# A graph network on one core: the back state turned through DRAM by VectorE, the engines' orders written anew, and some matmul operands moved by 32 bytes

## The chip, the cores and the metric

The kernel runs on 1 core of one Trainium2 chip (trn2), in one launch. The metric is the time of the device in microseconds, the median of its runs. All times below are microseconds (us) unless marked ns.

## What is computed

The input x holds 32 graphs of 256 nodes by 256 features (fp32), with one 256x256 adjacency matrix adj for all. Four layers follow each other, each with a residual and a layer norm over the features:

```
h = x
3 times:  a = adj @ h
          z = sigmoid([a, a] @ w3.T + b3 + h @ u3.T + bu)
          r = sigmoid([a, a] @ w4.T + b4 + h @ u3.T + bu)
          c = tanh([a, a] @ w5.T + b5 + (r * h) @ u5.T + bv)
          h = (1 - z) * h + z * c
x = norm(x + h)
rel = adj.T * (q @ k.T), each row divided by its length;  x = norm(x + rel @ v)     (q, k, v = x @ Wq.T, Wk.T, Wv.T)
x = norm(x + (adj @ x) @ w2 + b2)
x = norm(x + D adj D @ (x @ w3s) + b3s)                  (D = 1 / sqrt of the degrees)
```

## The kernel before

**Arithmetic.** Every fp32 operand of a large matmul is split into two parts of type float32r, hi (a ScalarE copy) and lo (operand minus hi, on VectorE, the functions ending in `_lo`). A product takes three matmuls per 128 rows of contraction: hi by hi, hi by lo, lo by hi. So a bank of PSUM (128x512 fp32) costs 6 matmuls of 512 columns (`base`, `reset`, `update`, `candidate_mixed`, `candidate_reset`: a 128x128 weight, a state of 512 columns streamed), or 12 of 256 columns (`mix`, `keys`, `values`, `relate`, `attend`, `mix_nodes`, `convolve`, where the 256 nodes or features of one graph are streamed). In the names of the profile, out<-a,b, a is what is streamed and b what is loaded as weight.

**Pairs and lanes.** The 32 graphs are worked on in 16 pairs, 512 nodes each. Two lanes are interleaved. The front lane runs two of the three rounds of a pair p (n = 2p and 2p+1 in the code), the back lane the third round of the pair before, q = p - 1, and then, as `main`, the layers of q. One pass of the loop `Fori(2, LAST)` is 13 times the same; a `start` and a `finish` stand around it. In `finish` the last pair's third round and its layers run in the front lane (`last_pair`).

**The state and its turning.** A round needs its state h twice: features on partitions (`feat`, for `base`) and nodes on partitions (`node`, for `mix`). `hand_over_h` leaves the new state of the back lane as `feat`; `turn_h(state_b, ...)` (L677) turns it by 8 TensorE transposes of 128x128 into a PSUM bank, from where `node_hi` (ScalarE) and `node_lo` (VectorE) split it. The front state of the odd rounds and the sum in front of the layers are turned another way: VectorE transposes 32x32 blocks (`turn_state`, `turn_sum_blocks`), SP writes them to a DRAM scratch and reads them back in another order (`move_blocks`, L370 and L373: one write, a wait for its landing, four reads), and `moved_hi` and `moved_lo` split what arrives.

**Order.** Each engine's instructions stand in a list written out by hand in its `body`, `start` and `finish`, and each engine works strictly through its own. They wait for each other by semaphores. SP issues nearly all DMAs, in its own order: `load_front`, `load_blocks`, `keep_input`, `move_sum`, `move_blocks`, `store`. TensorE's list in the loop, end of a pass and beginning of the next: `mix_nodes(main, q, 1, 0 and 1)`, `convolve(main, q, 1, 0)`, `turn_h(state_b, p, 0 and 1)`, `convolve(main, q, 1, 1)`, then `mix(back)`, `mix(front)`, `base(back)`, `reset(back)`. The last layer norm of a pair (`out_sum`, `stats_of(3)`, `moments_of(3)` on VectorE, `inverse_std` on GpSimd, `normalise_rows(3)` on ScalarE, then `store`) runs into the next pass.

**Addresses.** Tensors lie one behind the other in a partition, in the order in which the code declares them, each at a multiple of 32 bytes. Before the change every operand of every matmul starts at a multiple of 128 bytes. The 8 floats of `shift_32` move what is declared behind it by 32 bytes, until `shift_back`.

## Time and profile before

| what | value |
|---|---|
| median of 3 runs | 1224.64 us (1224.62 to 1224.92) |
| the profiled execution's own time | 1224.91 us |
| its span, first to last instruction | 1223.1 us |
| TensorE busy | 1207.9 us, 99% |
| VectorE busy | 1003.4 us, 82% |
| ScalarE busy | 657.5 us, 54% |
| GpSimd busy | 192.8 us, 16% |
| granted TensorE clock, mean | 0.998 |
| DMA | 66.93 MB, 18.2% of 16 engines on SP's queue |

The engines run beside each other, so busy shares don't add up; what counts is the engine whose work ends last at each place. PE is TensorE's matmuls, PEld its weight loads (they run beside the matmuls), DVE is VectorE, ACT ScalarE, POOL GpSimd, SP SyncE with its DMA queue. Matmuls overlap in the profile: the time one costs is the distance to the start of the next, not its duration.

### The profile page before, as it was taken

How to read it: one execution, taken by the hardware profiler on the slowest of the kernel's cores; microseconds unless marked ns; L12 is line 12 of the kernel's file. 1: busy time of each engine (PE TensorE's matmuls, PEld its weight loads, DVE VectorE, ACT ScalarE, POOL GpSimd, SP SyncE). 2: the span in 40 equal slices, each digit the busy share in tenths (PEclk: the TensorE clock that was granted, in tenths of full speed). 3: DMA queues.
4: the chain of work that ended last, by engine and by line, in shares of the span. 5: the costliest groups of instructions: out<-in, count | busy, mean ns of one | idle time of the engine just before them, and what ended most of it. 6: DMA issues, size and time to landing. Idle time of an engine off the chain costs nothing.

```text
span 1223.1 us, 21243 instructions
## 1 busy us (share of the span) xinstructions
PE 1207.9 (99%) x7454; PEld 1089.1 (89%) x7454; DVE 1003.4 (82%) x2220; ACT 657.5 (54%) x1179; POOL 192.8 (16%) x447
## 2 busy tenths in 40 slices
PE   9999999999999999999999999999999999999997
PEld 7789899898998989899898998989989898998896
DVE  7689788897878978788887888978789787886799
ACT  5455555555555555555555555555555555555542
POOL 1002021110211102012020211102111021120122
PEclk9999999999999999999999999999999999999999
DMA  6020221303113030120402213031130311300001
GB/s 207 18 84 21 63 77 35 103 0 86 51 34 103 0 103 34 46 91 1 119 17 53 84 34 103 0 86 51 34 103 0 103 34 42 95 1 35 1 2 35
DMA packets 105021, 66.93 MB, mean 55 GB/s; under 512 B 65690, under 2 KB 98468, under 8 KB 104996
## 3 DMA queue, kind: packets, MB, share of 16 engines
q1 hardware_dynamic: 104784, 66.08, 18.2%
q0 software_dynamic: 192, 0.52, 0.2%
q8 instruction: 15, 0.25, 0.1%
q14 instruction: 10, 0.08, 0.0%
q10 hardware_dynamic: 20, 0.01, 0.0%
HBM read 35.13 MB, written 23.07 MB: 48 GB/s over the span
## 4 chain that ended last, share of the span: by engine, by line
PE 97%; DVE 2%; POOL 0%; ACT 0%; issue 0%; DVEq 0%; POOLq 0%
PE b_ps L515 41%; PE f_ps L515 31%; PE f_ps L510 15%; PE b_ps L510 7%; PE f_ps L677 1%; PE b_ps L741 1%; PE b_ps L559 0%; PE f_ps L1052 0%; DVE b_stats L1678 0%; DVE f_stats L1678 0%; DVE f_gate L1694 0%; PE b_ps L574 0%; DVE hf_feat L1706 0%; DVE hf_feat L1694 0%; DVE normed L1694 0%
## 5 line engine op out<-in xcount | busy, mean ns | idle before, releaser
L423 POOL TENSOR_TENSOR b_var_eps<-b_moments,eps 128x2 f32<-128x2 f32 x120 | 34.9, 290 | 913.1 <-DVE b_moments L1685 913.0
L1115 ACT ACTIVATE f_cand<-f_ps,bias_c 128x512 f32<-128x512 f32 x66 | 45.6, 691 | 86.0 <-PE f_ps L515 84.3
L425 POOL TENSOR_TENSOR b_rstd<-b_var_eps,neg_half 128x2 f32<-128x2 f32 x120 | 88.2, 735 | 9.4
L1063 ACT ACTIVATE b_rh_hi<-b_ps 128x512 fp32r<-128x512 f32 x90 | 53.7, 596 | 65.5 <-PE b_ps L515 65.5
L1103 ACT ACTIVATE f_gate<-f_ps,bias_r 128x512 f32<-128x512 f32 x66 | 45.4, 688 | 70.7 <-PE f_ps L515 70.7
L1063 ACT ACTIVATE b_a_hi<-normed 128x512 fp32r<-128x512 f32 x60 | 37.9, 632 | 61.3 <-DVE normed L1694 61.3
L515 PE MATMUL f_ps<-adjT_hi,hf_node_hi 128*128 128x256 f32 x264 | 67.3, 287 | 0.5 <-DVE adjT_lo L1481 0.5
L515 PE MATMUL f_ps<-adjT_lo,hf_node_hi 128*128 128x256 f32 x264 | 66.1, 283 | 0.0
L1720 DVE TENSOR_TENSOR b_rh_lo<-b_ps,b_rh_hi 128x512 fp32r<-128x512 f32 x90 | 61.4, 682 | 4.6 <-ACT b_rh_hi L1063 4.4
L1577 DVE TENSOR_TENSOR f_cand<-f_z,f_cand 128x512 f32<-128x512 f32 x66 | 45.5, 689 | 23.0 <-ACT f_cand L1115 23.0
L1561 DVE TENSOR_TENSOR f_gate<-f_gate,hf_feat 128x512 f32<-128x512 f32 x66 | 44.8, 680 | 20.2 <-ACT f_gate L1103 20.2
L1063 ACT ACTIVATE f_a_hi<-f_ps 128x512 fp32r<-128x512 f32 x66 | 39.0, 592 | 40.5 <-PE f_ps L515 40.5
L1555 DVE TENSOR_TENSOR b_a_lo<-b_ps,b_a_hi 128x512 fp32r<-128x512 f32 x30 | 19.4, 687 | 49.2 <-ACT b_a_hi L1063 49.2
L1111 ACT ACTIVATE f_z<-f_ps,bias_z 128x512 f32<-128x512 f32 x66 | 45.1, 685 | 26.6 <-PE f_ps L510 26.6
L1555 DVE TENSOR_TENSOR f_a_lo<-f_ps,f_a_hi 128x512 fp32r<-128x512 f32 x66 | 44.9, 682 | 14.0 <-ACT f_a_hi L1063 14.0
L1182 ACT ACTIVATE result<-result,b_shift,b_rstd 128x256 f32<-128x256 f32 x56 | 30.8, 597 | 46.2 <-POOL b_shift L431 46.2
L1063 ACT ACTIVATE hf_feat_hi<-hf_feat 128x512 fp32r<-128x512 f32 x64 | 38.8, 626 | 25.1 <-DVE hf_feat L1641 22.2
L515 PE MATMUL f_ps<-hf_feat_hi,u3T_hi 128*128 128x512 f32 x132 | 52.0, 394 | 0.1
L515 PE MATMUL f_ps<-f_a_hi,w4T_hi 128*128 128x512 f32 x132 | 51.8, 393 | 0.0
L515 PE MATMUL f_ps<-hf_feat_hi,u3T_lo 128*128 128x512 f32 x132 | 51.8, 392 | 0.0
L515 PE MATMUL f_ps<-f_a_hi,w4T_lo 128*128 128x512 f32 x132 | 51.6, 391 | 0.0
L510 PE MATMUL f_ps<-f_a_hi,w34T_hi 128*128 128x512 f32 x132 | 51.5, 390 | 0.0
(340 smaller groups left out, 4335.7 us busy)
## 6 DMA issues: line engine op xcount, KB each, us to landing
x_front<-in_x SPq DMA_DIRECT2D x16, 512.0 KB, 4.0
x_blocks<-in_x SPq DMA_DIRECT2D x60, 128.0 KB, 2.9
input_t<-hf_feat SPq DMA_DIRECT2D x15, 512.0 KB, 2.9
turn_sum<-normed SPq DMA_DIRECT2D x14, 512.0 KB, 2.7
result<-turn_sum SPq DMA_DIRECT2D x56, 128.0 KB, 2.8
turn_f<-f_gate SPq DMA_DIRECT2D x14, 512.0 KB, 2.7
f_z<-turn_f SPq DMA_DIRECT2D x56, 128.0 KB, 2.8
out<-result SPq DMA_DIRECT2D x14, 512.0 KB, 3.2
```

Of the source, the lines that this page charges most:

```text
L423: pool.tensor_tensor(Y.var_eps[:, g], Y.moments[:, g, :, 1], eps[:], ALU.add).then_inc(Y.s_var, 1)
L425: pool.tensor_tensor(Y.rstd[:, g], Y.var_eps[:, g], neg_half[:], ALU.pow).then_inc(Y.s_rstd, 1)
L510: last = pe.matmul(bank, s, m, start=start and i == 0, stop=stop and i == len(terms) - 1, skip_group_check=True)
L515: return pe.matmul(bank, s, m, start=start, stop=stop, skip_group_check=True)
L1063: return act.activation(dst, src, ACT.Copy)
L1103: act.activation(L.gate[:, k], L.ps0[:, k], ACT.Sigmoid, bias=bias_r[:, k:k + 1]).then_inc(L.s_r, 1)
L1111: act.activation(L.z[:, k], L.ps0[:, k], ACT.Sigmoid, bias=bias_z[:, k:k + 1]).then_inc(L.s_z, 1)
L1115: act.activation(L.cand[:, k], L.ps1[:, k], ACT.Tanh, bias=bias_c[:, k:k + 1]).then_inc(L.s_tanh, 1)
L1555: dve.tensor_tensor(L.a_lo[:, k], L.ps1[:, k], full(L.a_hi[:, k]), ALU.subtract).then_inc(L.s_a_lo, 1)
L1561: dve.tensor_tensor(L.gate[:, k], L.gate[:, k], L.state.feat[:, k], ALU.mult).then_inc(L.s_rh, 1)
L1577: dve.tensor_tensor(L.cand[:, k], L.z[:, k], L.cand[:, k], ALU.mult).then_inc(L.s_zc, 1)
L1720: dve.tensor_tensor(lo[:, g], src, full(hi[:, g]), ALU.subtract).then_inc(done, 1)
```

## The change

The back state is turned like the front one: `turn_state(state_b)` on VectorE, `move_blocks(state_b)` through a scratch of its own on SP, `moved_hi` and `moved_lo` in place of `node_hi` and `node_lo`. `turn_h(state_b)` goes. Its blocks and what comes back lie in the back lane's `kept` and `cand`. The values v of the attention now lie in the back lane's a_hi and a_lo, and the operand x of the two convolutions gets a buffer of its own (it lay there before). adjT, norm_adjT, w2s, w3s, the split sum and the split relation are declared between `shift_32` and `shift_back`. And all engines' lists are written anew, in `body`, `start` and `finish`; the diff shows the loop's where the order around the turned state is, the rest only moves instructions. The front mix no longer waits for the back state to have left its bank, but for the tanh before it.

```diff
--- before.py
+++ after.py
...
-        if by_blocks:
-            self.s_blocks = sem(f"{name}_s_blocks")
-            self.s_written, self.s_moved = sem(f"{name}_s_written"), sem(f"{name}_s_moved")
+        self.s_blocks = sem(f"{name}_s_blocks")
...
-        adjT = split_matrix("adjT")
-        norm_adjT = split_matrix("norm_adjT")
...
-        w2s = split_matrix("w2s")
-        w3s = split_matrix("w3s")
...
 
-        state_f = State(sb, sem, "hf", [P, C, T], [P, G, C, D], True)
-        state_b = State(sb, sem, "hb", [P, C, T], [P, G, C, D], False)
+        state_f = State(sb, sem, "hf", [P, C, T], [P, G, C, D])
...
+        state_b.scratch = scratch("turn_b")
+        state_b.blocks, state_b.moved = quarters(back.kept), quarters(back.cand)
...
 
+        shift_32 = sb("shift_32", [P, 8])
+        adjT = split_matrix("adjT")
+        norm_adjT = split_matrix("norm_adjT")
+        w2s = split_matrix("w2s")
+        w3s = split_matrix("w3s")
+        sum_split = sb("sum_hi", [P, C, T], F32R), sb("sum_lo", [P, C, T], F32R)
+        rel_split = nodes("rel_hi", F32R), nodes("rel_lo", F32R)
+        shift_back = sb("shift_back", [P, 8])
+
         main = Layers(sb, sem, "b", back, per_graph, input_t, s_input_t, 0,
-                      (sb("sum_hi", [P, C, T], F32R), sb("sum_lo", [P, C, T], F32R)), nodes("normed"), nodes("result"),
-                      (nodes("v_hi", F32R), nodes("v_lo", F32R)), (nodes("rel_hi", F32R), nodes("rel_lo", F32R)),
+                      sum_split, nodes("normed"), nodes("result"),
+                      (per_graph(back.a_hi), per_graph(back.a_lo)), rel_split,
                       sb("sq_sum", [P, G, N]), True)
...
         main.sum_blocks, main.sum_moved = (t[:].rearrange("p g c d -> p (g c) d") for t in (main.normed, main.result))
+
+        main.x_hi, main.x_lo = nodes("x_hi", F32R), nodes("x_lo", F32R)
...
             keep_input(0)
+            move_blocks(state_b, 1)
             with sp.Fori(1, LAST) as p:
                 load_front(p + 1)
                 load_blocks(p + 1)
                 keep_input(p)
                 move_sum(main, p - 1)
                 move_blocks(state_f, p)
+                move_blocks(state_b, p + 1)
                 store(main, p - 1)
...
                     pe.wait_ge(main.s_ax_lo, conv(n - 1, 1, k))
-                if pair is not None and later(pair):
-                    pe.wait_ge(state_b.s_node_lo, upto(pair - 1, k))
+                if pair is not None:
+                    pe.wait_ge(front.s_tanh, upto(n - 1, k))
...
             def body(p, q):
 
                 for k in range(2):
+                    mix(front, 2 * p, k, p)
+                for k in range(2):
+                    base(back, q, k)
+                for k in range(2):
                     mix(back, q, k)
                 for k in range(2):
-                    mix(front, 2 * p, k, p)
-                for k in range(2):
-                    base(back, q, k)
-                for k in range(2):
                     reset(back, q, k)
-                candidate_mixed(back, q, 0)
                 for k in range(2):
                     update(back, q, k)
                 candidate_mixed(back, q, 1)
+                candidate_mixed(back, q, 0)
                 for k in range(2):
                     candidate_reset(back, q, k)
                 base(front, 2 * p, 0, p)
                 reset(front, 2 * p, 0)
                 base(front, 2 * p, 1, p)
+                update(front, 2 * p, 0)
                 reset(front, 2 * p, 1)
+                candidate_mixed(front, 2 * p, 0)
+                update(front, 2 * p, 1)
+                candidate_reset(front, 2 * p, 0)
                 candidate_mixed(front, 2 * p, 1)
-                update(front, 2 * p, 0)
-                candidate_mixed(front, 2 * p, 0)
-                candidate_reset(front, 2 * p, 0)
-                update(front, 2 * p, 1)
+                keys(main, q, 0)
                 candidate_reset(front, 2 * p, 1)
-                for k in range(2):
-                    keys(main, q, k)
-                values(main, q, 0)
-                for k in range(2):
-                    relate(main, q, k)
+                keys(main, q, 1)
+                relate(main, q, 0)
+                for k in range(2):
+                    values(main, q, k)
+                relate(main, q, 1)
                 base(front, 2 * p + 1, 0)
-                values(main, q, 1)
+                sum_squares(main, q, 0)
+                for k in range(2):
+                    attend(main, q, k)
+                sum_squares(main, q, 1)
                 base(front, 2 * p + 1, 1)
-                sum_squares(main, q, 0)
-                attend(main, q, 0)
-                sum_squares(main, q, 1)
                 for k in range(2):
                     mix(front, 2 * p + 1, k)
-                attend(main, q, 1)
-                reset(front, 2 * p + 1, 0)
+                mix_nodes(main, q, 0, 0)
+                for k in range(2):
+                    reset(front, 2 * p + 1, k)
+                convolve(main, q, 0, 0)
+                mix_nodes(main, q, 0, 1)
+                update(front, 2 * p + 1, 0)
+                convolve(main, q, 0, 1)
                 candidate_mixed(front, 2 * p + 1, 0)
-                reset(front, 2 * p + 1, 1)
-                mix_nodes(main, q, 0, 0)
-                update(front, 2 * p + 1, 0)
-                mix_nodes(main, q, 0, 1)
-                for k in range(2):
-                    convolve(main, q, 0, k)
                 candidate_reset(front, 2 * p + 1, 0)
+                update(front, 2 * p + 1, 1)
                 candidate_mixed(front, 2 * p + 1, 1)
-                update(front, 2 * p + 1, 1)
                 candidate_reset(front, 2 * p + 1, 1)
...
 
                 for k in range(2):
+                    moved_hi(state_b, q, k, q + 1)
+                input_hi(p, 0)
+                for k in range(2):
                     a_hi(back, q, k)
+                reset_gate(back, q, 0)
                 a_hi(front, 2 * p, 0)
-                reset_gate(back, q, 0)
+                reset_gate(back, q, 1)
                 rh_hi(back, q, 0)
-                reset_gate(back, q, 1)
-                input_hi(p, 0)
                 update_gate(back, q, 0)
                 rh_hi(back, q, 1)
                 update_gate(back, q, 1)
+                a_hi(front, 2 * p, 1)
...
                 conv_ax_hi(main, q, 0, 1)
                 rh_hi(front, 2 * p + 1, 1)
                 update_gate(front, 2 * p + 1, 0)
+                conv_x_hi(main, q, 1, 0)
+                input_nodes_hi(p + 1, 1)
                 candidate(front, 2 * p + 1, 0)
-                conv_x_hi(main, q, 1, 0)
                 update_gate(front, 2 * p + 1, 1)
                 conv_x_hi(main, q, 1, 1)
                 candidate(front, 2 * p + 1, 1)
                 for k in range(2):
                     conv_ax_hi(main, q, 1, k)
                 out_sum(main, q, 0)
-                node_hi(state_b, p, 0, 2 * p + 0 + 1)
-                feat_hi(state_b, p, 0)
-                node_hi(state_b, p, 1, 2 * p + 1 + 1)
-                feat_hi(state_b, p, 1)
-                input_nodes_hi(p + 1, 1)
+                for k in range(2):
+                    feat_hi(state_b, p, k)
                 out_sum(main, q, 1)
                 for k in range(2):
...
 
                 for k in range(2):
+                    moved_lo(state_b, q, k)
+                turn_blocks(p, 0)
+                for k in range(2):
                     a_lo(back, q, k)
                 a_lo(front, 2 * p, 0)
-                reset_h(back, q, 0)
-                turn_blocks(p, 0)
+                input_lo(p, 0)
+                for k in range(2):
+                    reset_h(back, q, k)
                 rh_lo(back, q, 0)
-                reset_h(back, q, 1)
-                input_lo(p, 0)
                 keep(back, q, 0)
+                rh_lo(back, q, 1)
                 residual(main, back, q, q, 0)
-                rh_lo(back, q, 1)
                 turn_blocks(p, 1)
+                keep(back, q, 1)
                 input_lo(p, 1)
                 a_lo(front, 2 * p, 1)
                 candidate_part(back, q, 0)
...
                 candidate_part(front, 2 * p + 1, 0)
-                normalise(main, q, 2, 1)
-                conv_x_lo(main, q, 1, 0)
+                keep(front, 2 * p + 1, 1)
                 hand_over_h(p, 0)
                 conv_x_lo(main, q, 1, 1)
-                fill(main, q, 1, 0)
+                turn_state(state_b, p, 0)
                 candidate_part(front, 2 * p + 1, 1)
-                keep(front, 2 * p + 1, 1)
+                hand_over_h(p, 1)
+                turn_state(state_b, p, 1)
                 conv_ax_lo(main, q, 1, 0)
-                hand_over_h(p, 1)
                 fill(main, q, 1, 1)
                 conv_ax_lo(main, q, 1, 1)
+                input_nodes_lo(p + 1, 0)
                 stats_of(main, q, 3, 0)
-                for k in range(2):
-                    node_lo(state_b, p, k)
-                for k in range(2):
-                    input_nodes_lo(p + 1, k)
-                feat_lo(state_b, p, 0)
                 moments_of(main, q, 3, 0)
-                feat_lo(state_b, p, 1)
+                input_nodes_lo(p + 1, 1)
                 stats_of(main, q, 3, 1)
                 moments_of(main, q, 3, 1)
+                for k in range(2):
+                    feat_lo(state_b, p, k)
...
```

## Rows read from the trace of the kernel before

**Rows 1.** The page: TensorE's line, and the chain that ended last by engine
```profile
PE 1207.9 (99%) x7454; PEld 1089.1 (89%) x7454; DVE 1003.4 (82%) x2220; ACT 657.5 (54%) x1179; POOL 192.8 (16%) x447
...
PE 97%; DVE 2%; POOL 0%; ACT 0%; issue 0%; DVEq 0%; POOLq 0%
```

**Rows 2.** Windows: stretch, us, busy by engine (instructions), granted clock, DMA, GB/s
```profile
498.30:572.65 74.35, 74.35 (x462) 67.19 (x461) 61.64 (x136) 40.96 (x76) 11.90 (x28) 1.00 0.19 56
...
1093.13:1223.10 129.97, 119.58 (x770) 108.10 (x768) 104.74 (x253) 57.23 (x102) 23.30 (x48) 0.99 0.05 17
```

**Rows 3.** Timeline, TensorE: start, duration, line, out<-streamed,weight, form
```profile
499.74 0.28 PE L515 MATMUL b_ps<-adjT_hi,hb_node_hi 128*128 128x256 f32 x1
...
500.70 0.64 PE L515 MATMUL b_ps<-adjT_hi,hb_node_lo 128*128 128x256 f32 x4
...
510.89 0.39 PE L510 MATMUL b_ps<-b_a_hi,w34T_hi 128*128 128x512 f32 x1
...
514.97 0.39 PE L515 MATMUL b_ps<-b_rh_hi,u5T_hi 128*128 128x512 f32 x1
```

**Rows 4.** Timeline, TensorE: 512 columns behind a 256 block, and the end
```profile
578.41 0.40 PE L515 MATMUL b_ps<-hb_feat_hi,u3T_hi 128*128 128x512 f32 x1
...
579.80 0.39 PE L515 MATMUL b_ps<-hb_feat_hi,u3T_hi 128*128 128x512 f32 x1
```

**Rows 5.** Timeline, TensorE: 256 columns behind 512
```profile
553.44 0.28 PE L515 MATMUL b_ps<-adjT_hi,b_a_hi 128*128 128x256 f32 x1
553.55 0.28 PE L515 MATMUL b_ps<-adjT_lo,b_a_hi 128*128 128x256 f32 x1
```

**Rows 6.** Timeline, TensorE: the back state's turning and what follows
```profile
570.35 1.04 PE L677 MATMUL f_ps<-ident,hb_feat 128*128 128x128 f32 x8
571.15 0.36 PE L515 MATMUL b_ps<-w3s_hi,b_rh_hi 128*128 128x256 f32 x1
571.35 0.28 PE L515 MATMUL b_ps<-w3s_lo,b_rh_hi 128*128 128x256 f32 x1
```

**Rows 7.** Timeline, TensorE: the product in full precision at the start
```profile
27.28 1.89 PE L574 MATMUL b_ps<-hb_feat 128*128 128x256 f32 x8
```

**Rows 8.** Timeline, TensorE, ending: convolve behind mix_nodes; in brackets idle time, releaser
```profile
1189.10 0.74 PE L515 MATMUL b_ps<-adjT_hi,b_a_lo 128*128 128x256 f32 x4 [0.22 <-DVE b_a_lo L1720]
1190.62 0.36 PE L515 MATMUL b_ps<-w2s_hi,b_rh_hi 128*128 128x256 f32 x1 [0.78 <-ACT b_rh_hi L1063]
```

**Rows 9.** Timeline, VectorE and SP's queue: the front state's way through DRAM
```profile
534.25 0.70 DVE L1621 STREAM_TRANSPOSE f_gate<-hf_feat 128x512 f32<-128x512 f32 x1
...
534.98 0.34 SPq L370 DMA_DIRECT2D turn_f<-f_gate  x1
537.66 1.73 SPq L373 DMA_DIRECT2D f_z<-turn_f  x4
```

**Rows 10.** The page's DMA issues: KB each, us from issue to landing
```profile
f_z<-turn_f SPq DMA_DIRECT2D x56, 128.0 KB, 2.8
```

**Rows 11.** Timeline, TensorE and ScalarE behind the pass's last candidate_reset
```profile
566.04 0.28 PE L515 MATMUL b_ps<-norm_adjT_hi,b_a_hi 128*128 128x256 f32 x1
...
566.24 0.69 ACT L1115 ACTIVATE f_cand<-f_ps,bias_c 128x512 f32<-128x512 f32 x1
```

**Rows 12.** Groups by line, ScalarE, one pass: busy us, mean ns
```profile
L1063 ACT ACTIVATE b_a_hi<-b_ps 128x512 fp32r<-128x512 f32 x2 | 1.1, 580 | 0.0
```

**Rows 13.** Timeline, VectorE, GpSimd, ScalarE: the last norm, second graph
```profile
575.92 0.75 DVE L1678 BATCH_NORM_STATS2 b_stats<-result 128x6 f32<-128x256 f32 x2
...
577.21 0.19 POOL L423 TENSOR_TENSOR b_var_eps<-b_moments,eps 128x2 f32<-128x2 f32 x1
...
578.64 1.10 ACT L1182 ACTIVATE result<-result,b_shift,b_rstd 128x256 f32<-128x256 f32 x2 [0.25 <-POOL b_shift L431]
```

**Rows 14.** Timeline, TensorE, start: base(back, 0)
```profile
48.39 0.47 PE L515 MATMUL b_ps<-hb_feat_hi,u3T_hi 128*128 128x512 f32 x1 [1.39 <-ACT hb_feat_hi L1063]
```

**Rows 15.** Windows, start: columns as in rows 2
```profile
50.00:53.00 3.00, 3.00 (x10) 2.51 (x11) 1.83 (x3) 0.71 (x2) 0.00 (x0) 0.50 0.01 3
```

879 lines of the change are left out of this document (440 added, 439 removed).

## The prediction, made before the change was run

> **What bounds the kernel now.** I read the page's totals first: TensorE is busy 99% of the span and carries 97% of the chain that ended last [rows 1]. Then the windows by stage: one pass of the loop takes 74.35 us and TensorE is busy for all of it, VectorE for 61.6, ScalarE for 41.0; only the ending (130.0 us, 119.6 busy) has holes [rows 2]. So in the 13 passes the time is the number of matmuls times the spacing of their starts, and nothing else. The timeline gives that spacing (durations overlap, so only starts count): eight matmuls of 256 columns in 0.96 us, 120 ns each; 18 of 512 columns in 4.08 us, 226.7 ns each [rows 3]. [...] A pass holds, by the code, 264 matmuls of 256 columns (three mix calls of two banks, then keys, values, relate, attend, two of mix_nodes, two of convolve: 22 banks of 12) and 180 of 512 (30 products of 6), 31.7 + 40.8 us. The rest of the 74.35 is the back state's turning, the sums of squares and small costs where the length changes: the first six matmuls of 512 columns behind a 256 block take 1.39 us instead of 1.36 [rows 4], and the first of 256 behind a 512 block has a spacing of 0.11 instead of 0.12 [rows 5].
>
> **The change, part by part.**
>
> *The removed transposes.* `turn_h(state_b)` is 8 transposes at the end of a pass: from the first, 570.35, to the next block, 571.15, 0.80 us, and that block's first spacing is 0.20 instead of 0.12 [rows 6]. Together 0.88, less 0.01 for the slightly tighter ones behind it: **-0.87 us a pass**. There is nothing else on TensorE there, so all of it is on the path.
>
> *The addresses.* adjT, norm_adjT, w2s, w3s, sum and relation move to addresses 32 bytes off a multiple of 64; everything else stays on one. In each of main's 256-column products exactly one of the two operands moves: mix, mix_nodes and convolve stream a shifted matrix past an unshifted weight, keys streams the shifted sum, values, relate and attend load a shifted weight. In all 512-column products neither moves. No row has a matmul with operands placed so, so the effect has to be bounded. [...] I take the better row that exists for 256 columns, one step less: 264 x 6.67 = **-1.76 us a pass** (ends -2.85 and +1.76, and 0 is possible).
>
> [...]
>
> *The order.* Lengths change 8 times a pass instead of 6 (base back, reset back, candidate_reset front 1, the base of the odd round twice, reset, update, candidate): 2 x 0.027 less one or two gains of 0.007: **+0.05**. More important is what stands behind `mix(back, 1)`: before, mix and base of other states (5.6 us), now `reset(back, 0)` at once, which needs a_hi and a_lo of the last bank. The nearest row is in the ending, where convolve stands straight behind mix_nodes: four matmuls from 1189.10, 0.74 long, the last lasting about 0.28 and so starting near 1189.56; next start 1190.62 behind one ScalarE copy [rows 8]; less its own 0.12 that is 0.94 us from where TensorE could have gone on. Here bank 0's two products (0.45) fit in, bank 1's start at 0.94 instead of 0.45; then a_lo of bank 1 is due at 1.7 (0.20 from matmul to ScalarE, 0.58 for the copy [rows 11, 12], 0.7 on VectorE, 0.2 to start), where the stream gets at 1.62, and the rest of the product follows it. **+0.57 us a pass** (from 0.4, if the copy is quicker, to 0.75, since `input_hi(p, 0)`, behind `turn_blocks`, now stands ahead of both a_hi on ScalarE). This is a new wait, and behind it in TensorE's list stand only `reset(back, 1)` and the updates, which need the same values.
>
> *The back state through DRAM.* VectorE gets two transposes of 0.70 [rows 9], moved_lo takes node_lo's place: 61.6 + 1.4 = 63 of some 72.5 us, not the bound. Two more terms matter, both against the time at which TensorE gets to `mix(back, 0)`. Let T be the end of a pass's matmuls. From T come mix(front) 24 x 0.12 and base(back) 2.75: T + 5.6 (5.5 with the shift). (i) The turn. The front state's, now: the transpose ends at 534.95, the write is issued at 534.98, the four reads within 1.73 from 537.66, and one lands 2.8 us after its issue [rows 9, 10]: the last at about 541.9, 7.0 us after the transpose. The back's starts when the last candidate_reset ends, 5.8 us before T (566.04; tanh at 566.24 for 0.69 [rows 11]), then candidate_part, hand_over and transpose at 0.6 to 0.7 each, behind conv_x_lo and the other half's transpose: 2.9 to 3.6 us. So it has landed at T + 4.1 to 4.8 and node_hi is there at T + 4.8 to 5.5. (ii) ScalarE's queue. `moved_hi(back)` is behind `normalise_rows(q, 3)`. Now these end at T + 7.1 (578.64 + 1.10 against 572.65), because VectorE gets to the last stats only at 575.92 [rows 13]; from there to the end it is 3.8 us. In the new order only input_nodes_lo, stats and moments stand before it: T + 1.2, so moved_hi can start at about T + 4.8. Both just fit; I count **+0.2 us a pass**, from 0 to 0.8 (the faster the matmuls, the less cover: with the surcharge gone T comes 0.6 earlier against the turn).
> SP is passed in order: `move_blocks(state_b)` waits ahead of `store` and the next x_front load, but store waited for the later normalise_rows anyway; its five transfers fall into a time without others. x_front is needed only late in the pass.
>
> *Start and ending.* [...] After: a turn of about 10.7 us against mix(front), prepare, candidate_mixed and base (7.4), and one reset wait; without the eight transposes. About the same, -1. Outside the loop 696 more matmuls are shifted (last_pair's keys to attend are not): -4.6, 1 of it lost in the ending's holes.
>
> *Sum.* 13 x (-0.87 - 1.76 + 0.05 + 0.57 + 0.2) = -23.5; -1 - 3.6: -28.1 against the profiled execution's own 1224.9 (span 1223.1 and 1.8 around it; the runs' median is 0.3 less): **1196.5 us**.
>
> **The rivals.**
> A, above: 1196.5 (own range 1189 to 1205), 0.42. For it: the spacings move both ways where the length changes [rows 4, 5].
> [...] 0.22.
> C, the addresses do nothing: 13 x -0.25 - 1: 1220.5, between 1216 and 1226. For it: every operand in the trace starts at a multiple of 128 bytes, and halves of a tensor 512 bytes apart show the same 120. [...] 0.20.
> D, one step more: 13 x 1.51 + 4.6 - 1: 1248. 0.07.
> E, the other side: `moved_hi(back)` is late, in ScalarE's queue. If the last normalise_rows end where they do now, T + 7.1, node_hi is there at 7.7 and TensorE waits 2.25 us instead of 0.2: 1226 with A's addresses, 1247 with C's. It decides from 0.4 us a pass under C, 2.35 under A. For it: the chain goes over three engines [rows 13]. Against: the stats now stand ahead of what held them. 0.09.
>
> Faster or slower by over 0.2% (2.4 us, what a measurement of this kernel can tell from no change): faster A, B and 0.14 of C, 0.78; within 0.06 of C and 0.03 of E, 0.09; slower D and the rest of E, 0.13. The range 1182 to 1227 leaves out D, most of E and a little below B.
>
> **What the changed profile would show.** A pass of 72.5 us; no ident,hb_feat rows in the loop; starts of 256 columns 113 ns apart (109 in B, 120 in C, 127 in D), of 512 still 227; a hole of about 0.5 us before b_ps<-b_a_hi,w4T in each pass and nearly none before b_ps<-adjT,hb_node; ScalarE's hb_node_hi<-b_cand starting 4.8 us after the last convolve. I'd be wrong if the spacing stays at 120, or if that copy starts later than 6.

## The result and the profile after: slower by 0.5%

The kernel after takes 1231.04 us (1230.67 to 1231.56), the kernel before 1224.92 beside it: ratio 1.0051, 95% interval 1.0036 to 1.0065. Forecast were 1196.5 us and a range from 1182 to 1227, so the time lies outside the range and on the other side.

First the page of the kernel after: TensorE's totals, and the chain that ended last by engine.

```profile
PE 1204.4 (98%) x7334; PEld 1067.1 (87%) x7334; DVE 1022.4 (83%) x2250; ACT 667.2 (54%) x1179; POOL 222.2 (18%) x447
...
PE 79%; DVE 11%; POOL 4%; ACT 3%; issue 2%; ACTq 0%; DVEq 0%; POOLq 0%
```

TensorE does 120 instructions fewer than in [rows 1] and is busy 3.5 us less, yet its share of the last chain falls from 97% to 79%: the other engines now hold it up. The windows, with the columns of [rows 2], are one pass (from one end of the last convolve to the next) and the ending:

```profile
500.40:575.22 74.82, 74.29 (x454) 65.84 (x453) 62.89 (x139) 41.75 (x75) 14.00 (x28) 1.00 0.23 70
1098.66:1229.22 130.56, 119.16 (x770) 107.02 (x768) 104.75 (x254) 57.29 (x102) 25.50 (x48) 0.99 0.06 21
```

A pass was busy from end to end [rows 2] and now has 0.5 us of holes (more are inside, since a matmul of 256 columns is recorded with 0.28 us at a spacing of 0.12 [rows 3]). Over the 13 passes the mean goes from 74.35 to 74.77 us, 5.4 in all (the third and later ones: 74.78); the start takes 126.7 for 126.5 and the ending 0.6 more. That is the whole 6.1.

The starts of TensorE's matmuls, averaged over the passes from the third on, split the pass. A spacing more than 20 ns over its usual 120 or 227 counts as a wait, the rest as spacing:

```
us a pass                                 before   after   change  forecast
8 transposes                                0.79    0       -0.79   -0.87
256 columns, spacing over 120 ns           -0.06   -0.60    -0.54   -1.76
512 columns, spacing over 226.67 ns         0.17    0.26    +0.09   +0.05
wait in and in front of the reset           0       0.53    +0.53   +0.57
wait before and in mix(back)                0       0.80    +0.80   +0.20
last convolve                               0.08    0.28    +0.20    0
other waits                                 0.17    0.31    +0.14    0
sum                                                         +0.43   -1.81
```

So the transposes, the order's lengths and the reset came as forecast (of the 0.87 for the transposes, 0.08 is the slow spacing behind them, which the table has before in the row of the last convolve). Two terms did not: 32 bytes are worth a third of what I gave them, and the waits grow by 1.68 us a pass instead of 0.77.

**The spacing.** TensorE's timeline after, in the columns of [rows 3], a product of the last mix_nodes:

```profile
570.69 0.28 PE L525 MATMUL b_ps<-norm_adjT_hi,x_hi 128*128 128x256 f32 x1
...
571.63 0.64 PE L525 MATMUL b_ps<-norm_adjT_hi,x_lo 128*128 128x256 f32 x4
...
572.11 0.28 PE L525 MATMUL b_ps<-w3s_hi,b_rh_hi 128*128 128x256 f32 x1
```

Twelve starts from 570.69 to 572.11 are 118 ns each, where [rows 3] have 120. It is not uniform: where the weight starts 32 bytes ahead of the stream (mix, keys, the convolves) the means are 116.8 to 117.3, where it starts 32 bytes behind (values, relate, attend, and mix_nodes) 118.1 to 118.7. mix_nodes belongs to the second kind because `shift_back` is a second gap and puts nothing back: x_hi and x_lo, declared behind both, stand 64 bytes off, the matrices 32. So two operands moved there, where I had counted one.

**The wait before mix(back, 0).** The timelines of TensorE, ScalarE, SP's queue, VectorE and GpSimd around it, a pass's matmuls ending at T = 575.22:

```profile
581.53 0.36 PE L525 MATMUL b_ps<-adjT_hi,hb_node_hi 128*128 128x256 f32 x1 [0.47 <-ACT hb_node_hi L1067]
...
577.97 1.09 ACT L1186 ACTIVATE result<-result,b_shift,b_rstd 128x256 f32<-128x256 f32 x2 [1.90 <-POOL b_shift L441]
579.78 1.09 ACT L1186 ACTIVATE result<-result,b_shift,b_rstd 128x256 f32<-128x256 f32 x2 [0.71 <-POOL b_shift L441]
580.78 1.14 ACT L1067 ACTIVATE hb_node_hi<-b_cand 128x512 fp32r<-128x512 f32 x2
...
575.16 1.73 SPq L381 DMA_DIRECT2D b_cand<-turn_b  x4
...
576.28 0.74 DVE L1682 BATCH_NORM_STATS2 b_stats<-result 128x6 f32<-128x256 f32 x2
...
577.16 0.15 DVE L1689 BATCH_NORM_AGGREGATE b_moments<-b_stats 128x2 f32<-128x6 f32 x1
577.22 1.26 DVE L1613 TENSOR_TENSOR hb_feat_lo<-hb_feat,hb_feat_hi 128x512 fp32r<-128x512 f32 x2
...
575.86 0.55 POOL L433 TENSOR_TENSOR b_var_eps<-b_moments,eps 128x2 f32<-128x2 f32 x1 [9.89 <-DVE b_moments L1689]
...
577.41 0.52 POOL L441 TENSOR_TENSOR b_shift<-b_neg_mean,b_rstd 128x2 f32<-128x2 f32 x1
577.89 0.64 POOL L433 TENSOR_TENSOR b_var_eps<-b_moments,eps 128x2 f32<-128x2 f32 x1
...
579.54 0.20 POOL L441 TENSOR_TENSOR b_shift<-b_neg_mean,b_rstd 128x2 f32<-128x2 f32 x1
```

Read it backwards. TensorE starts at 581.53 on the first half of hb_node_hi. That copy starts at 580.78, T + 5.56, right behind the second normalise_rows, which had waited 0.71 for GpSimd. The last stats came when forecast (576.28, T + 1.06), but GpSimd was on the first graph's four operations until 577.89, 0.6 us after the second graph's moments were there, and then took 1.85 for its own. The four reads of the blocks were issued by 576.9, and nothing in ScalarE's row names a DMA. This is rival E's mechanism: ScalarE's queue, not the way through DRAM.

GpSimd is late because its own small operations are longer than before. The same b_shift of the first graph, in the trace of the kernel before:

```profile
577.06 0.20 POOL L431 TENSOR_TENSOR b_shift<-b_neg_mean,b_rstd 128x2 f32<-128x2 f32 x1
```

It takes 0.52 after, and the second graph's b_var_eps takes 0.64 for the 0.19 of [rows 13]: 0.77 us together, which is all by which the stretch from the last stats to the end of the norm has grown (3.82 to 4.59). What stands beside them is new: the order now has hb_feat_lo on VectorE right behind the moments, where VectorE was idle before. In the trace after, each of the 100 b_var_eps and b_shift that are longer than 0.23 us ends 0.03 to 0.07 us behind a VectorE operation with two inputs in SBUF, and none of the 76 short ones (0.20) starts while one runs. That it is the two hb_feat_lo that hold GpSimd up is my reading of these rows. No run moves them, so it is not tested, and that the wait would go with them is not shown.

**The reset, and the last convolve.** TensorE and ScalarE behind mix(back, 1), then TensorE and VectorE in the last convolve:

```profile
584.54 0.50 PE L525 MATMUL b_ps<-b_a_hi,w4T_hi 128*128 128x512 f32 x1
...
585.36 0.50 PE L525 MATMUL b_ps<-b_a_hi,w4T_hi 128*128 128x512 f32 x1
...
583.37 0.63 ACT L1067 ACTIVATE hf_feat_hi<-hf_feat 128x512 fp32r<-128x512 f32 x1 [1.46 <-DVE hf_feat L1645]
583.91 0.58 ACT L1067 ACTIVATE b_a_hi<-b_ps 128x512 fp32r<-128x512 f32 x1
584.71 0.60 ACT L1067 ACTIVATE b_a_hi<-b_ps 128x512 fp32r<-128x512 f32 x1 [0.22 <-PE b_ps L525]
...
573.09 0.73 PE L525 MATMUL b_ps<-w3s_hi,b_rh_lo 128*128 128x256 f32 x4
...
571.75 0.71 DVE L1625 STREAM_TRANSPOSE b_kept<-hb_feat 128x512 f32<-128x512 f32 x1
572.39 0.65 DVE L1724 TENSOR_TENSOR b_rh_lo<-b_ps,b_rh_hi 128x512 fp32r<-128x512 f32 x1
```

The two starts on b_a_hi are 0.82 apart where two matmuls need 0.45. Bank 1 starts 0.85 behind the end of the mix's spacing (584.51), forecast 0.94, and its a_hi waited for TensorE alone: this is the new neighbour. The a_hi of bank 0 is late as well: mix(back, 0) had ended near 583.3, and it starts only at 583.91, behind input_hi (the hf_feat_hi row), which had waited 1.46 for VectorE. Here it is still in time (it ends at 584.49, TensorE starts at 584.54). In the convolve b_rh_lo is made by 573.04, since the second turn_state stands ahead of it on VectorE; its four matmuls from 573.09 last 0.73 instead of 0.63.

### The profile page after: what moved, and what is told of

It is laid out like the page before. It is cut to its first block, busy times and chain, and to the rows that moved or that the text cites. A ratio compares the mean times of both kernels' runs of the same rounds, so it can differ in the third digit from the quotient of the medians.

```text
span 1229.2 us, 21109 instructions
## 1 busy us (share of the span) xinstructions
PE 1204.4 (98%) x7334; PEld 1067.1 (87%) x7334; DVE 1022.4 (83%) x2250; ACT 667.2 (54%) x1179; POOL 222.2 (18%) x447
## 4 chain that ended last, share of the span: by engine, by line
PE 79%; DVE 11%; POOL 4%; ACT 3%; issue 2%; ACTq 0%; DVEq 0%; POOLq 0%
PE b_ps L525 30%; PE f_ps L525 26%; PE f_ps L520 14%; PE b_ps L520 7%; POOL b_rstd L435 2%; DVE b_rh_lo L1724 2%; POOL b_var_eps L433 1%; DVE b_stats L1682 1%; DVE f_cand L1581 1%; DVE hb_feat L1587 1%; DVE b_kept L1625 1%; DVE b_ps L1719 1%; POOL b_shift L441 1%; PE b_ps L751 1%; ACT f_cand L1119 1%
## 5 line engine op out<-in xcount | busy, mean ns | idle before, releaser
L433 POOL TENSOR_TENSOR b_var_eps<-b_moments,eps 128x2 f32<-128x2 f32 x120 | 56.1, 468 | 859.2 <-DVE b_moments L1689 859.2
L435 POOL TENSOR_TENSOR b_rstd<-b_var_eps,neg_half 128x2 f32<-128x2 f32 x120 | 93.5, 779 | 9.4
L1067 ACT ACTIVATE x_hi<-normed 128x512 fp32r<-128x512 f32 x60 | 37.9, 631 | 74.0 <-DVE normed L1698 74.0
L1634 DVE TENSOR_TENSOR hb_node_lo<-b_cand,hb_node_hi 128x512 fp32r<-128x512 f32 x30 | 19.5, 689 | 42.2 <-ACT hb_node_hi L1067 42.2
L1569 DVE TENSOR_TENSOR f_rh_lo<-f_gate,f_rh_hi 128x512 fp32r<-128x512 f32 x66 | 44.8, 680 | 10.5 <-ACT f_rh_hi L1067 10.3
L520 PE MATMUL f_ps<-f_a_hi,w5T_hi 128*128 128x512 f32 x132 | 51.6, 391 | 1.8 <-DVE f_a_lo L1559 1.8
L525 PE MATMUL f_ps<-f_rh_hi,u5T_lo 128*128 128x512 f32 x132 | 51.6, 391 | 0.0
```

What stands on the lines that cost most here:

```text
L433: pool.tensor_tensor(Y.var_eps[:, g], Y.moments[:, g, :, 1], eps[:], ALU.add).then_inc(Y.s_var, 1)
L435: pool.tensor_tensor(Y.rstd[:, g], Y.var_eps[:, g], neg_half[:], ALU.pow).then_inc(Y.s_rstd, 1)
L520: last = pe.matmul(bank, s, m, start=start and i == 0, stop=stop and i == len(terms) - 1, skip_group_check=True)
L525: return pe.matmul(bank, s, m, start=start, stop=stop, skip_group_check=True)
L1067: return act.activation(dst, src, ACT.Copy)
L1569: dve.tensor_tensor(L.rh_lo[:, k], L.gate[:, k], full(L.rh_hi[:, k]), ALU.subtract).then_inc(L.s_rh_lo, 1)
```

## Experiments

Ratios are to the kernel before, timed beside each run; a mean pass is that of the 13.

### e1: the kernel after without the 32 bytes

```diff
-        shift_32 = sb("shift_32", [P, 8])
+        shift_32 = sb("shift_32", [P, 32])
...
-        shift_back = sb("shift_back", [P, 8])
+        shift_back = sb("shift_back", [P, 32])
```

> The kernel after with the two gaps 128 bytes wide, so that every matmul operand starts at a multiple of 128 bytes again and nothing else changes. Theory 1 (the 32 bytes are worth what the trace after seems to show, about 2.4 ns of each 256-column matmul where no wait lies between, 0.6 us a pass and 1.7 outside the loop): starts of 256 columns 120 ns apart again, and, since slower matmuls hide 0.1 of the wait for the back state, 1231.0 + 13 x 0.5 + 1.7 = 1239. Rival (the tighter starts come from the new order, the addresses do nothing): 1231 and a spacing of 117 to 118 as in the kernel after.

Measured: 1235.93 us (ratio to before 1.0085, 1.0071 to 1.0099), 4.9 above the kernel after. A pass is 75.11. The spacing is mixed, 115 to 123, with a mean of 119.4, where I expected 120 throughout. So the addresses do gain, and less here than expected (1239), for two reasons: at 128 bytes, the distance here, the spacing lies between (e13), 1.8 ns above the kernel after and not 2.5; and the waits of a pass are 0.18 us shorter beside the slower matmuls. Order and turning without the 32 bytes cost 11 us against before, 75.11 for 74.35 a pass. Which of the two costs it is not separated by any run.

### e2: the kernel before with the 32 bytes

```diff
-        adjT = split_matrix("adjT")
-        norm_adjT = split_matrix("norm_adjT")
...
-        w2s = split_matrix("w2s")
-        w3s = split_matrix("w3s")
...
+        shift_32 = sb("shift_32", [P, 8])
+        adjT = split_matrix("adjT")
+        norm_adjT = split_matrix("norm_adjT")
+        w2s = split_matrix("w2s")
+        w3s = split_matrix("w3s")
+        sum_split = sb("sum_hi", [P, C, T], F32R), sb("sum_lo", [P, C, T], F32R)
+        rel_split = nodes("rel_hi", F32R), nodes("rel_lo", F32R)
+        shift_back = sb("shift_back", [P, 8])
```

> The kernel before with the declarations moved as in the change, 32 bytes off, and no other edit. Theory 1: spacing 117 to 118, 0.55 us a pass and 1.9 outside, 1224.9 - 9 = 1216. My prediction's step, one 6.7 ns step for each matmul: 1224.9 - 26 = 1199. Rival, the addresses do nothing: 1225.

Measured: 1215.02 us, ratio 0.9913 (0.9899 to 0.9926). The windows of one pass and of the ending:

```profile
494.60:568.29 73.69, 73.69 (x463) 66.49 (x461) 61.61 (x136) 40.87 (x76) 11.88 (x28) 1.00 0.19 57
1084.39:1213.63 129.24, 118.58 (x770) 107.11 (x768) 104.70 (x253) 57.00 (x102) 23.21 (x48) 0.99 0.05 17
```

Nothing else has changed against [rows 2], and a mean pass is 0.63 us shorter: 2.5 ns for each of the 256-column matmuls (117.3 for 119.8 on average), nothing for the others. Outside the loop it is worth 0.6 in the start and 0.7 in the ending, 1.3 instead of the 3.6 forecast. This part alone makes the kernel faster; the step of 6.7 ns did not come.

### e3: moved_hi(back) between the two last normalise_rows

```diff
-                for k in range(2):
-                    normalise_rows(main, q, 3, k)
+                normalise_rows(main, q, 3, 0)
+                for k in range(2):
+                    moved_hi(state_b, p, k, p + 1)
+                normalise_rows(main, q, 3, 1)
```

(and the same at the end of `start`; the two moved_hi at the head of `body` and in `finish` go.)

> The kernel after with ScalarE's two moved_hi of the back state between the two last normalise_rows, not behind both. Theory 2 (the wait before mix(back, 0), 0.58 to 0.63 us a pass, is ScalarE's queue: the moved blocks had landed at 579.32, the copy started at 580.78): the wait goes, 1231.0 - 13 x 0.6 = 1223, and hb_node_hi starts at most 0.3 us behind the last landing. Rival (the way through DRAM is the bound): the copy starts no earlier than now, 1231. Second rival: normalise_rows is now late and with it a_hi(back), so the wait comes back in front of reset: 1228 to 1231.

Measured: 1221.74 us, ratio 0.9971 (0.9960 to 0.9982), 9.3 less than the kernel after, and faster than before. A mean pass is 73.96, 0.81 less. ScalarE's timeline and TensorE's, a pass's matmuls ending at 570.55:

```profile
573.31 1.09 ACT L1186 ACTIVATE result<-result,b_shift,b_rstd 128x256 f32<-128x256 f32 x2 [1.90 <-POOL b_shift L441]
574.76 1.15 ACT L1067 ACTIVATE hb_node_hi<-b_cand 128x512 fp32r<-128x512 f32 x2 [0.36 <-DMA b_cand<-turn_b]
575.82 1.08 ACT L1186 ACTIVATE result<-result,b_shift,b_rstd 128x256 f32<-128x256 f32 x2
...
576.24 0.28 PE L525 MATMUL b_ps<-adjT_hi,hb_node_hi 128*128 128x256 f32 x1
576.36 0.28 PE L525 MATMUL b_ps<-adjT_lo,hb_node_hi 128*128 128x256 f32 x1
```

Now the releaser is the DMA: the blocks are there at T + 4.2, inside the forecast 4.1 to 4.8, the copy starts at once, and TensorE, which gets there at T + 5.7, doesn't wait. Nor does the wait come back in front of the reset, the second rival: that one is 0.53 us a pass as in the kernel after. One place in ScalarE's list was worth 9 us, 3 more than the change lost by all.

### e4: the back lane's reset by halves

```diff
-                for k in range(2):
-                    reset(back, q, k)
+                reset_by_halves(back, q)
+                candidate_mixed(back, q, 1)
                 for k in range(2):
                     update(back, q, k)
-                candidate_mixed(back, q, 1)
...
+            def reset_by_halves(L, n):
+                for k in range(2):
+                    pe.wait_ge(L.s_a_hi, upto(n, 0))
+                    weights_by_high(L.ps0[:, k], columns(w4T, k), mixed(L), 0)
+                    pe.wait_ge(L.s_a_lo, upto(n, 0))
+                    weights_by_low(L.ps0[:, k], columns(w4T, k), mixed(L), 0)
...
```

The lines left out do the same for the second half, bank by bank, and signal s_reset.

> The kernel after with the back lane's reset in another order in the loop: the products of the first half of a (three of each bank, 1.36 us) ahead of those of the second half, and candidate_mixed(back, 1) ahead of the updates. Theory 3 (the 0.50 us a pass in front of and in the reset is the wait for a_hi and a_lo of the second half, and enough other work covers it): 1231.0 - 13 x 0.5 = 1224.5, all spacings in the reset 227 to 240. Rival (the chain from the mix over ScalarE and VectorE back to the gates is what counts, so the wait turns up at the updates or at candidate_reset): 1229 to 1231.

Measured: 1229.12 us, ratio 1.0031 (1.0019 to 1.0043), 1.9 less than the kernel after: a pass gains 0.15 of the 0.53. ScalarE's and VectorE's timelines behind mix(back, 0), which ends near 507.7:

```profile
507.86 0.63 ACT L1079 ACTIVATE hf_feat_hi<-hf_feat 128x512 fp32r<-128x512 f32 x1 [1.46 <-DVE hf_feat L1657]
508.40 0.58 ACT L1079 ACTIVATE b_a_hi<-b_ps 128x512 fp32r<-128x512 f32 x1
509.22 0.60 ACT L1079 ACTIVATE b_a_hi<-b_ps 128x512 fp32r<-128x512 f32 x1 [0.24 <-PE b_ps L525]
...
509.01 1.53 DVE L1571 TENSOR_TENSOR b_a_lo<-b_ps,b_a_hi 128x512 fp32r<-128x512 f32 x2 [1.18 <-ACT b_a_hi L1079]
```

The work that was put in between needs a_lo of the first half, and that starts only at 509.01 because a_hi stood behind input_hi. The theory (0.5 us a pass) failed. The time is in the rival's range (1229 to 1231), but not by its mechanism: the 0.39 that are left stand in the reset itself, none at the updates or candidate_reset. e14 takes up input_hi.

### e14: the same, with a_hi(back) ahead of input_hi

```diff
-                input_hi(p, 0)
                 for k in range(2):
                     a_hi(back, q, k)
+                input_hi(p, 0)
```

> The kernel of e4 (reset by halves) with a_hi(back, 0 and 1) ahead of input_hi(p, 0) in ScalarE's list. Theory: in e4 the first a_hi started 0.8 us late behind input_hi, which waits for VectorE's turning of x_blocks, and the halves had to wait for a_lo; now both are there and 0.45 of the 0.50 us a pass in the reset go: 1231.0 - 13 x 0.45 = 1225. Rival (the time returns at the updates or candidate_reset, or at the front lane's reset, whose input_hi is later now): 1228 to 1229 as e4.

Measured: 1224.18 us, ratio 0.9994 (0.9985 to 1.0003), 4.9 less than e4 and 6.9 less than the kernel after. ScalarE's timeline:

```profile
505.95 0.60 ACT L1079 ACTIVATE b_a_hi<-b_ps 128x512 fp32r<-128x512 f32 x1 [1.40 <-PE b_ps L525]
507.35 0.60 ACT L1079 ACTIVATE b_a_hi<-b_ps 128x512 fp32r<-128x512 f32 x1 [0.80 <-PE b_ps L525]
507.85 0.62 ACT L1079 ACTIVATE hf_feat_hi<-hf_feat 128x512 fp32r<-128x512 f32 x1
```

Both copies now wait for TensorE alone, 1.4 us apart, the length of a mix; the reset's starts are about 230 ns apart, and with both edits 0.54 of the pass is back, as the theory had it (1225). In the kernel after the wait was that of the new neighbour; the place of input_hi bites once the halves ask for a_lo of bank 0 early. a_hi ahead of input_hi without the halves was not run.

### e8: all waits mended at once

e3, e4 and e14 together, and on VectorE `conv_ax_lo(main, q, 1, 0)` ahead of `turn_state(state_b, p, 1)`.

> The kernel after with the waits that its trace shows mended at once: moved_hi(back) ahead of the last normalise_rows; the reset by halves; on ScalarE a_hi(back) ahead of input_hi(p, 0), which held it up for 0.8 us behind the turning of x_blocks; on VectorE conv_ax_lo(1, 0) ahead of the second turn_state(back). Theory (each wait goes by itself, no other takes its place): from 1221.7 less 13 x (0.5 + 0.25) = 1212. Rival (the waits are one chain, and what is taken out at one place comes back at the next): 1217 to 1221.

Measured: 1215.08 us, ratio 0.9925 (0.9912 to 0.9939). A mean pass is 73.42, 1.35 less than after; by e3 and e14 alone 0.81 + 0.54 = 1.35. The two large waits are independent, and they sum. The move on VectorE adds nothing to that: the convolve's wait falls from 0.28 to 0.17 where I had expected it to go, and 0.07 comes back as small waits in mix(back). So 1215 lies between the theory (1212) and its rival (1217 to 1221). The ending is 131.9, 1.3 longer than after and 2.0 longer than before. Against e2, which has the same 32 bytes and still turns by TensorE (1215.02), there is nothing gained: 0.31 us a pass is won and given back in the ending.

### e5 to e7: which distance, which operands

e5: gaps of 64 bytes in place of 32, in the kernel of e2. e6: the kernel before with one gap of 32 bytes ahead of all matrices. e7: e2 with w34T, w4T, w5T, u3T and u5T declared inside the gap too.

> The kernel before with the declarations moved as in the change, but 64 bytes off in place of 32. Theory A (what counts is whether the streamed operand and the weight start at the same place within 64 bytes): nothing is gained, 1225 and a spacing of 120. Rival B (any distance between the two that is no multiple of 128 bytes helps, or just their new places in the partition): 1215 to 1218 as with 32 bytes.

> The kernel before with one gap of 32 bytes ahead of all matrices, so that every operand of the large matmuls starts 32 bytes off, streamed and weight alike. Theory A (the distance between the two operands counts): 1225, spacing 120. Rival B (it is enough that an operand doesn't start at a multiple of 64): 1215 or less; then the 512-column products are tighter too, and up to 180 x 2.5 ns a pass more is gained, 1209.

> The kernel before with the 32 bytes as in the change, and the weights of the 512-column products (w34T, w4T, w5T, u3T, u5T) moved with the rest, so that in all large products but last_pair's exactly one operand is 32 bytes off. Theory A: the 512-column matmuls get about 2.5 ns each as well, 224 ns apart, 1215 - 13 x 0.45 - 1 = 1208. Rival (in these the load of the next weight ends long before the stream does and does not matter): 226.7 as before and 1215.

Measured: e5 1216.80 us (ratio 0.9929, 0.9916 to 0.9943), e6 1224.97 (1.0000, 0.9991 to 1.0009), e7 1230.31 (1.0044, 1.0030 to 1.0058). A pass of each, e5, e6 and e7 in this order:

```profile
494.57:568.29 73.72, 73.72 (x462) 66.52 (x461) 61.58 (x136) 40.88 (x76) 11.91 (x28) 1.00 0.19 57
```

```profile
496.94:571.30 74.36, 74.36 (x463) 67.21 (x461) 61.61 (x136) 40.89 (x76) 11.91 (x28) 1.00 0.19 56
```

```profile
499.26:573.92 74.66, 74.66 (x462) 66.50 (x461) 61.63 (x136) 41.04 (x76) 11.90 (x28) 1.00 0.19 56
```

With every operand moved alike (e6) nothing changes at all (1224.97 us, 256 columns at 119.8 ns as before): it is the distance between the streamed operand and the weight that counts. 64 bytes do as well as 32 in the loop (73.72 for 73.73 us a pass), against theory A. And a distance of 32 in the 512-column products costs some 6.5 ns each where they ran at 226.7 (the mean of all 180 is 233.2 for 227.7 in e2, +0.98 us a pass), against both theories of e7. In e5 relate alone had 113.3 ns, the level I had forecast for all.

### e9 to e12: a signed distance for all products

Further gaps place the matrices, sum and relation, and wqk so that in every 256-column product the weight is the same number of bytes behind the stream.

> The kernel before with four gaps of 64 bytes so placed that in every 256-column product of the loop the loaded weight starts 64 bytes behind the streamed operand (modulo 512), and in every 512-column product at the same place. So far the spacing went by that signed distance: 0 gave 120 ns, -32 (the matrices streamed, 32 off) 116.9, +32 118.2, -64 117.8, and +64, which only relate had in e5, 113.3. Theory A' (it is a matter of this signed distance alone): all at 113.3, 261 x 6.5 ns = 1.7 us a pass, 1224.9 - 13 x 1.7 - 4 = 1199, the time that my prediction gave this part. Rival (relate is a case of its own, by its banks or by which operand it streams): 1214 to 1217.

> The mended kernel of e8 with the addresses of e9. Theory A': 1215.1 - 13 x 260 x (117.5 - 113.3) ns - 2 = 1199, if TensorE doesn't now run into the turn through DRAM; a pass of e8 less 1.1 us. Rival (the faster matmuls give cover away, and the waits of e8, 0.56 us a pass, grow by as much): 1206 to 1213.

> The kernel before with the weight 96 bytes behind the stream in the 256-column products, and 32 bytes ahead of it (-32) in the 512-column ones. Theory A' modulo 128: 96 is as -32, 256 columns at 116.9, and 512 columns at -32 gain 3 ns where +32 lost 6.5 (e7): 1224.9 - 13 x (0.8 + 0.5) - 3 = 1205. Theory A' modulo 512: 96 is a place of its own, anything from 113 to 120. Rival for 512 columns (each distance but 0 costs as +32 did): 227 + 6.5, 1216 + 15 = 1231.

> The kernel before with the weight 128 bytes behind the stream in the 256-column products, and 64 bytes behind it in the 512-column ones. If the pattern repeats every 128 bytes, 256 columns are at 120 as before; if only modulo 512, they may be at any level. For 512 columns +64: by the 256 columns' pattern 6.5 ns less each (220, 1224.9 - 13 x 1.2 = 1209); by e7's +32, 6.5 ns more (1224.9 + 15 = 1240).

```
                                us       ratio (interval)          pass    256 columns, ns  512 columns, ns
e9   before, +64             1210.63  0.9878 (0.9863 to 0.9893)   73.48   116.6            227.4
e10  e8, +64                 1209.58  0.9871 (0.9856 to 0.9886)   73.03   116.2            227.5
e11  before, +96; 512: -32   1235.10  1.0078 (1.0064 to 1.0092)   74.99   118.4            233.1
e12  before, +128; 512: +64  1235.44  1.0084 (1.0069 to 1.0098)   75.13   118.9            233.1
```

e9 is 15 us faster than before, e10 hardly to be told from it; neither reaches 1199. e10 is in its rival's range (1206 to 1213), but for another reason: its waits grow by 0.07 us a pass only, and the spacing falls by 1.5 ns and not by 4.2. At the one distance of 64 there are two levels: in e9 relate and the first convolve run at 113.3 to 113.8, mix(back) and the first mix_nodes at 117.8 and 118.3; in e10 values is at 113.3 and that convolve at 117.8. So the distance alone does not set the spacing, and theory A' falls. e11 and e12 are slower, near what their rivals had (1231 and 1240), for the 512-column products.

### e13: the distances by themselves

It leaves the graph network out: blocks of matmuls from two tensors, the weight's column offset growing by 16 bytes. One execution, granted clock 1.00 throughout these blocks.

> No graph network: after a warm-up of 256 matmuls of 512 columns, blocks of 16 float32r matmuls of 256 columns (two streams in turn, each pair with a new weight, as in mix), with the weight 0, 16, 32, ... 496 bytes behind the stream; the same in falling order; the same with 6 matmuls of 512 columns ahead of each block; and blocks of 12 matmuls of 512 columns at each distance. The output is a copy of a few sums and no result of the network. Theory A' (the distance alone sets the spacing): each distance has one spacing in all three series, 120 at 0, 117 to 118 at +32 and -32, and 113 to 118 at +64; 512 columns 227 at 0 and 233 elsewhere. Rival (history: at some distances there are two stable spacings, and what stood before the block chooses): the series differ at the same distance by 4 to 5 ns, at 64 most likely.

The same 15 starts of 256 columns at a distance of 64, in the rising and in the falling series (TensorE's timeline):

```profile
75.20 1.87 PE L61 MATMUL ps<-stream,weight 128*128 128x256 f32 x15
...
184.55 1.93 PE L61 MATMUL ps<-stream,weight 128*128 128x256 f32 x15
```

The last lasts 0.28, so 14 spacings are 1.59 and 1.65 us: 113.6 and 117.9 ns. Means of each block without its first four spacings, in ns; from 256 on it repeats within 0.3, but for the falling series at 448 (113.3), 496 (117.3), 416 and 480 (0.5 off), and 512 columns at 256 (226.7):

```
distance, bytes            0    16    32    48    64    80    96   112   128   144   160   176   192   208   224   240
256 columns, rising    120.0 118.3 118.5 117.9 113.4 118.7 117.5 120.4 118.7 120.0 119.2 118.3 117.7 116.8 116.4 117.5
256 columns, falling   119.8 118.1 118.3 117.9 117.7 118.6 118.7 120.5 118.5 120.1 119.9 118.4 117.7 116.7 117.0 119.8
256, behind 512        120.0 118.3 118.1 118.4 117.8 118.6 118.5 120.5 120.2 119.1 119.5 117.9 117.8 116.5 116.5 117.3
512 columns            227.3 226.7 233.6 233.1 232.9 232.3 234.3 233.3 233.9 233.6 233.0 229.1 228.4 233.3 233.3 226.7
```

The distance sets most of it, with a period of 256 bytes, and history the rest: 64 and 192 have a second level at 113.3 that a block keeps once it is in it. The change's own distances are in the table: -32 (224) 116.5, +32 118.1 to 118.5, as read in its trace; and e1's 128 gives 118.5 to 120.2 (119.4 in its trace), less than the 120 of distance 0: one of the two reasons why taking the 32 bytes out cost less there than putting them in gained in e2.

## Why the prediction was wrong, point by point

**What bounds the kernel, the transposes, the lengths, the reset.** TensorE's starts were the right measure, and these three terms came out at -0.87 (0.79 and the 0.08 behind them) for -0.87, +0.09 for +0.05 and +0.53 for +0.57. In the reset the mechanism was right too, a copy of ScalarE behind the last matmul of the mix.

**The addresses: the step mis-sized.** The step that failed is "I take the better row that exists for 256 columns, one step less: 264 x 6.67". That it counts whether one of the two operands moves was right (e2: 1215.0; both moved, e6: 1225.0). The sign was a guess between two rows [rows 4, 5], and in part luck: at 512 columns the same 32 bytes cost 6.5 ns (e7). The better row was a first spacing behind another length (0.11, [rows 5]), and the level at which a block settles at 32 bytes is another: 116.5 or 118.3 (e13), -0.54 us a pass instead of -1.76. That is 16 of the 34 us between forecast and result. No run shows the step of 6.67 ns at 32 bytes, nor the -2.85 us a pass of the one end (109 ns): at 32 bytes the runs showed 116.4 to 118.5 (e13) for 120.0 at 0, and the shortest anywhere was 113.3. That level exists at 64 and 192 bytes and not always. If the place of the operands made no difference, e2, e6 and e7 would all be 1225. They are 1215.0, 1225.0 and 1230.3, with float32r and a load in every matmul; what it is in the chip that makes the difference is not shown.

**The waits: the second step.** "moved_hi can start at about T + 4.8" failed: T + 5.56. (T + 1.2 and 3.8 us are T + 5.0, a slip of 0.2 in the sum.) The step behind it was "from there to the end it is 3.8 us" [rows 13]. I had carried this time over from the kernel before, where VectorE is idle beside GpSimd's operations; in the new order hb_feat_lo stands there, two of them take 0.77 us longer, and the stretch is 4.6. The blocks were in time (T + 4.2, e3). Counted was 0.2, the bound was 0.8, measured 0.80. This is rival E's queue, with chance 0.09, at a third of its price (2.25), and not by its condition: the last norm ends at T + 5.65, not at T + 7.1. With the addresses' small gain it brings a pass back to about where it was (-0.79 - 0.54 + 0.09 + 0.53 + 0.80 = +0.09); the rest is small waits that I had put at nothing. The 0.20 in the last convolve, where turn_state stands ahead of conv_ax_lo, I had named as a delay of the transpose and not as one of b_rh_lo; with the other small waits it is 0.34, uncounted. All waits together are 12 us of the 34.

**Start and ending.** Forecast -4.6, measured +0.8. The start, put at -1, takes 0.2 more (126.7 for 126.5). The 32 bytes give 1.3 there (e2) in place of 3.6. The rest, about 2 us, comes with the new lists and the turning in `start` and `finish`; which part is open, no run here tells it. It is more than 2, since the clock hides some of it. In the traces of before and of e2 the granted clock is at 0.50 for 3.4 us of the start, from 49.9 and 51.0 on [rows 15]. In such a stretch the starts of 512 columns are 0.43 us apart (before, 50.55 to 51.83) for 0.23, and those of 256 columns 0.21 (e6, 1192.39 to 1195.16) for 0.12. In the trace after it stays at 1.00, first row below, which I had not expected. e6, which has before's order and spacing, lacks the stretch too, and its start takes 125.2 us for 126.5. So at the same clock the start after is 1.5 longer, not 0.2. The windows of after, of e6 and of e10, with the columns of [rows 2]:

```profile
49.90:53.30 3.40, 1.64 (x11) 1.27 (x10) 2.78 (x6) 2.13 (x4) 0.00 (x0) 1.00 0.38 154
...
1192.00:1195.40 3.40, 3.40 (x19) 3.40 (x18) 2.79 (x12) 0.60 (x1) 1.21 (x3) 0.50 0.00 0
...
1083.00:1086.40 3.40, 3.40 (x9) 2.62 (x10) 2.87 (x5) 1.23 (x3) 0.00 (x0) 0.51 0.85 308
```

The same explains part of the endings. e6's takes 131.2 for before's 130.0 and has such a stretch at 1192.0; e10's takes 133.1 for the 131.9 of e8 and has one at 1083.0, where e8 has none. That e8's ending takes 1.3 more than the kernel after's, with no such stretch, is seen and not explained.

**The rivals.** C (the addresses do nothing) is excluded by e2; B (109 ns) and D (127 ns) by the spacings, 117.6 after. The result is A's mechanism at a third of its size with E's wait at a third of its price, and E's line has that wait only with A's whole gain or with none. Its price with A's addresses is wrong by its own terms as well: 1196.5 and 13 x 2.05 are 1223, not 1226. The two signs of being wrong (spacing still 120, copy later than T + 6) did not come, 117.6 and 5.56; both terms missed by less than the signs asked for, and together by 28 us.

## What to carry to other kernels

A wait in front of the bounding engine was here twice one place in another engine's list: look for what the late instruction stood behind, and whether its operand was already there (moved_hi: 0.81 us a pass for one place in a list; a_hi, with the reset by halves: 0.54). A time carried over from the kernel before did not hold once other work stood beside it, on the engine next to it (hb_feat_lo beside GpSimd, 0.77 us). Before an engine is relieved of work (here 0.8 us of transposes), add up what its successor needs at the seam, on every engine, since each new wait there was about as large (0.53 and 0.80). And when an effect has never been measured, take a run of it alone before its size is multiplied by 3,400.

## What was not expected of the hardware

The spacing of float32r matmuls with a weight load each went by the distance in the partition between weight and stream, with a period of 256 bytes but for the exceptions named in e13: 256 columns from 113.3 to 120.5 ns, 512 columns from 226.7 to 234.3. The two lengths want different distances: 32 bytes behind gained 1.5 to 1.9 ns at 256 columns (e13) and cost some 6.5 at 512 (e7, e13). At 64 bytes there were two levels, 113.3 and 117.8 (e9, e13). In the trace after, GpSimd's b_var_eps and b_shift (128x2) took 0.20 us in 76 cases and 0.23 to 0.65 in 100, and each of the 100 ended 0.03 to 0.07 us behind the end of a VectorE operation with two inputs in SBUF. Gaps of a few hundred bytes, placed as in e9, took 1.2% off the kernel before (e9); with the mended change it is 1.3% (e10, 1209.58 us). These two are the fastest here; what separates them (1210.63 and 1209.58) is within the noise.
